# Expert rows of a two-layer kernel: loaded as exchanged 32x32 blocks and turned by VectorE, tags in loads of their own

## The reference

```python
logits = xn @ moe_gate_w + moe_gate_b
topw, topi = jax.lax.top_k(logits, K)                      # 2 of 8 experts per token
topw = jax.nn.softmax(topw, axis=-1)
w_dense = jnp.sum(jax.nn.one_hot(topi, E) * topw[..., None], axis=-2)
h = _gelu(jnp.einsum('bsd,edh->ebsh', xn, ew1) + eb1[:, None, None, :])
eo = jnp.einsum('ebsh,ehd->ebsd', h, ew2) + eb2[:, None, None, :]
moe_out = jnp.einsum('ebsd,bse->bsd', eo, w_dense)
```

## Time and profile before

| | |
|---|---|
| median of 3 runs | 793.02 us (789.99 to 794.43) |
| the profiled execution | 790.34 us |
| its span | 788.4 us |
| busy in the span | TensorE 84%, VectorE 75%, ScalarE 57%, GpSimd 31% |
| first load of a tile issued | 496.64 us |
| `up` of the last tile starts | 719.3 us |

### The profile page before, as it was taken

One profiled execution on the slowest core, in us unless ns is written; L12 is line 12 of the kernel. 1 busy time (PEld: TensorE's weight loads), 2 busy tenths in 40 slices (PEclk: granted clock), 3 DMA queues, 4 the chain that ended last, 5 costly groups with the idle time before them and its releaser, 6 DMA issues. The chain is left out here.

```text
span 788.4 us, 16245 instructions
## 1 busy us (share of the span) xinstructions
PE 662.5 (84%) x4681; PEld 491.2 (62%) x4682; DVE 592.2 (75%) x1649; ACT 452.1 (57%) x868; POOL 244.9 (31%) x295
## 2 busy tenths in 40 slices
PE   5799579999899989989997999599999999999000
PEld 4685335647465564746554687488888889887000
DVE  5836878889797988989789779376767767675493
ACT  3126357573746557384664744467676766765287
POOL 2000202121706335080523354033434333334132
PEclk9999799999999999999998999799999999999555
DMA  4603325253453635335662583454334444220783
GB/s 135 204 0 115 53 80 82 80 108 112 135 115 111 121 121 115 100 111 121 226 125 67 163 282 109 123 149 142 109 116 144 141 145 145 84 82 17 229 280 133
DMA packets 81775, 99.11 MB, mean 126 GB/s; under 512 B 7728, under 2 KB 71867, under 8 KB 81596
## 3 DMA queue, kind: packets, MB, share of 16 engines
q1 hardware_dynamic: 65308, 68.81, 27.9%
q0 software_dynamic: 16416, 29.67, 15.9%
HBM read 62.42 MB, written 33.68 MB: 122 GB/s over the span
## 5 line engine op out<-in xcount | busy, mean ns | idle before, releaser
L1678 POOL DMA_INDIRECT scratch_ys<-ye,place x78 | 83.0, 1064 | 159.7 <-ACT ye L1724 147.8
L52 PE MATMUL bank<-words 128*128 128x512 bf16 (+1 forms) x576 | 109.5, 345 | 8.4 <-DVE words L946 7.4
L52 PE MATMUL down<-words,h_s_e 128*128 x936 | 110.2, 274 | 1.0 <-DVE yb L1799 0.8
L52 PE MATMUL up<-xe_s,words 128*128 128x256 bf16 x936 | 110.1, 275 | 0.9 <-DVE xe_s L1815 0.9
L52 PEld LDWEIGHTS up<-xe_s,words 128*128 x936 | 92.3, 99 | 12.2 <-issue 1.3
L52 PEld LDWEIGHTS down<-words,h_s_e 128*128 128x128 bf16 x936 | 91.2, 98 | 13.9 <-issue 1.5
L52 PE MATMUL bank<-xn_s,mlp_w 128*128 128x512 bf16 x384 | 88.0, 387 | 8.1 <-DVE xn_s L720 8.1
L52 PEld LDWEIGHTS bank<-words 128*128 128x128 bf16 x576 | 55.3, 98 | 56.2 <-DVE words L946 9.1
L462 POOL DMA_INDIRECT scratch_zs<-rows,pos x64 | 73.4, 1147 | 44.3 <-DVE pos L1034 25.5
L52 PE MATMUL bank<-mlp_w,shared 128*128 128x256 bf16 x768 | 86.4, 273 | 0.0
L400 POOL TENSOR_TENSOR rs<-mv,eps_t 128x4 f32<-128x4 f32 x16 | 5.0, 310 | 246.5 <-DVE mv L710 246.5
(11 more groups left out here) (239 smaller groups left out, 1213.4 us busy)
## 6 DMA issues: line engine op xcount, KB each, us to landing
xr<-scratch_zs SPq DMA_DIRECT2D x39, 264.0 KB, 2.9
words<-scratch_ys SPq DMA_DIRECT2D x16, 514.0 KB, 8.8
scratch_abel<-staged SPq DMA_DIRECT2D x8, 514.0 KB, 3.7
abel_all<-scratch_abel SPq DMA_DIRECT2D x8, 514.0 KB, 5.9
x_in<-in_x SPq DMA_DIRECT2D x8, 512.0 KB, 4.9
words<-in_out_b_row SPq DMA_DIRECT2D x8, 512.0 KB, 3.6
x_res<-in_mlp_b_row SPq DMA_DIRECT2D x8, 512.0 KB, 3.6
words<-in_x POOLq DMA_DIRECT2D x8, 512.0 KB, 7.9
```

The lines of the kernel that those rows point to most:

```text
L52: last = nc.tensor.matmul(dst, lhs(a, k), rhs(b, k), start=start and n == 0, stop=stop and n == total - 1)
L1678: nc.gpsimd.indirect_dma_start(out=ys_dram[:, :], out_offset=bass.IndirectOffsetOnAxis(ap=place[:, k, s:s + 1], axis=0), in_=ye[:, k % 2, ...
```

## The change

SyncE loads the data columns of a tile by eight DMAs in place of one. Each takes 32 of the 256 columns for all 256 rows into 32 partitions, as 8 blocks of 32x32, each of which stands where its turned version has to be, but is itself not yet turned. Each contiguous piece is 128 bytes. VectorE then turns all blocks of the tile in one operation (`turned`), into `xt` in SBUF; TensorE's four transposes and their two PSUM banks are gone. VectorE does `turned(q + 2)` at the head of step q.

The tags of four tiles are loaded by four DMAs of their own (`load_tags`), issued right behind the load of every fourth tile, and VectorE makes weights and places of four tiles in one go, in five operations of 128x8, at every fourth step. The buffers for weights and places hold eight tiles, and the loop steps by eight tiles in place of four (4 rounds in place of 8), with `load_branch` twice in it. SyncE waits for `e_xT_done` ahead of a tile and for `e_placed` ahead of tags.

```diff
-        xr = sb("xr", [P, 4, ST, ROW])
+        SQ, GROUP, RING = 32, 4, 8
+        xb = sb("xb", [P, 4, KC, SLOT])
+        xt = sb("xt", [P, 2, KC, SLOT])
+        tags = sb("tags", [P, 2, GROUP, ST, ROW - D])
...
                 row = sp.value_load(tile_row[0:1, bass.ds(q, 1)], min_val=0, max_val=NE * REGION - SLOT)
                 wait(sp, xT_done, q - 3)
-                wait(sp, weight_r, q - 3)
-                wait(sp, placed, q - 3)
-                sp.dma_start(xr[:, k], zs_dram[bass.ds(row, SLOT), :].rearrange("(s p) c -> p s c", p=P))\
-                    .then_inc(zs_in[k], 16)
+                blocks = zs_dram[bass.ds(row, SLOT), 0:D].rearrange("(b j) (k a i) -> a k j b i", j=SQ, k=KC, i=SQ)
+                for a in range(P // SQ):
+                    for c in range(KC):
+                        sp.dma_start(xb[a * SQ:(a + 1) * SQ, k % 4, c].rearrange("j (b i) -> j b i", i=SQ), blocks[a, c])\
+                            .then_inc(zs_in[k % 4], 16)
+                if k % GROUP == 0:
+                    load_tags(q, k // GROUP)
+
+            def load_tags(q, g):
+
+                for n in range(group_size(q)):
+                    row = sp.value_load(tile_row[0:1, bass.ds(q + n, 1)], min_val=0, max_val=NE * REGION - SLOT)
+                    if n == 0:
+                        wait(sp, placed, q - GROUP)
+                    sp.dma_start(tags[:, g, n], zs_dram[bass.ds(row, SLOT), D:ROW].rearrange("(s p) c -> p s c", p=P))\
+                        .then_inc(tags_in[g], 16)
...
-                    nc.scalar.activation(xe[:, k % 2, c], turn_bank[k % 2][:, c], ACT.Identity, bias=beta[:, c:c + 1],
+                    nc.scalar.activation(xe[:, k % 2, c], xt[:, k % 2, c], ACT.Identity, bias=beta[:, c:c + 1],
...
+            def turned(q, k):
+                dve.wait_ge(zs_in[k % 4], (q - k % 4) * 32 + 128)
+                wait(dve, xe_r, KC * (q - 1))
+                nc.vector.transpose(xt[:, k % 2].rearrange("p k n -> p (k n)"),
+                                    xb[:, k % 4].rearrange("p k n -> p (k n)")).then_inc(xT_done, 1)
...
             def body(q, k):
                 if isinstance(q, int) and q == 0:
+                    turned(0, 0)
+                    turned(1, 1)
                     tails(0, 0)
-                places(q, k)
+                if not (isinstance(q, int) and q >= QT - 2):
+                    turned(q + 2, (k + 2) % RING)
+                if k % GROUP == 0:
+                    places(q, k)
...
-            def turned_rows(q, k):
-                pe.wait_ge(zs_in[k], (q - k) * 4 + 16)
-                wait(pe, xe_r, KC * (q - 1))
-                for s in range(ST):
-                    for c in range(KC):
-                        last = nc.tensor.transpose(turn_bank[k % 2][:, c, s * P:(s + 1) * P],
-                                                   xr[:, k, s, c * P:(c + 1) * P], ident[:, :])
-                last.then_inc(xT_done, 1)
-
...
-                if isinstance(q, int) and q == 0:
-                    turned_rows(0, 0)
-                if not (isinstance(q, int) and q == QT - 1):
-                    turned_rows(q + 1, (k + 1) % 4)
                 up(q, k, expert_of(q))
```

More of the change, by code:

```diff
@@ L1581, in experts @@
         xe_s = sb("xe_s", [P, 2, 2 * KC, SLOT], BF16)
-        is_first, more, at = sb("is_first", [P, 4, ST]), sb("more", [P, 4, ST]), sb("at_e", [P, 4, ST])
-        weight = sb("weight", [P, 4, ST])
-        place = sb("place", [P, 4, ST], U32)
+        is_first, more, at = [sb(n, [P, GROUP, ST]) for n in ("is_first", "more", "at_e")]
+        weight = sb("weight", [P, RING, ST])
+        place = sb("place", [P, RING, ST], U32)
         h_s = sb("h_s_e", [P, 2, 2, FC, SLOT], BF16)
@@ L1620, in experts, with group_size @@
         assert TAIL // 4 - 1 == BATCHES
+        def group_size(q):
+            return min(GROUP, QT - q) if isinstance(q, int) else GROUP
         def over_tiles(eng, body, first=0, last=QT, every_four=lambda q: None):
[L1625 to L1630, removed]
+            for q in range(first, GROUP):
+                body(q, q)
+            with eng.Fori(GROUP, TAIL - RING + 1, RING) as q:
+                for k in range(RING):
+                    if k % GROUP == 0:
+                        every_four(q + k)
+                    body(q + k, (GROUP + k) % RING)
             for q in range(TAIL, last):
-                body(q, q % 4)
+                body(q, q % RING)
         @block.sync
@@ L1788, in places, with each @@
-                dve.wait_ge(at_r, q + 1)
-                nc.vector.scalar_tensor_tensor(place[:, k], at[:, k], float(NTILES * P),
-                                               nowhere[:, bass.ds(q, 1)].rearrange("p a s -> p (a s)"), ALU.add,
-                                               ALU.max).then_inc(placed, 1)
+                    return tags[:, g, 0:N, :, c - D:c - D + 1].bitcast(dt).rearrange("p q s a -> p q (s a)")
+                def each(v):
+                    return v.rearrange("p (q a) -> p q a", a=1).to_broadcast([P, N, ST])
@@ new lines, in places @@
+                at_k = slice(k, k + N)
+                dve.wait_ge(tags_in[g], (q - k) * 8 + 16 * N)
+                if not (isinstance(q, int) and q < RING):
+                    for n in range(4):
+                        dve.wait_ge(ys_out[n], (q - RING) * 4 * ST + 16 * ST)
+                nc.vector.tensor_tensor(is_first[:, 0:N], tag(FIRST, I32), each(tef[:, bass.ds(q, N)]), ALU.is_equal)\
+                    .then_inc(first_r, GROUP)
+                dve.wait_ge(first_r, q + GROUP)
+                nc.vector.tensor_tensor(more[:, 0:N], is_first[:, 0:N], tag(MORE_W, F32), ALU.mult)\
+                    .then_inc(more_r, GROUP)
```

46 lines of the change are left out of this document (22 added, 24 removed).

## The result

The changed kernel takes a median of 828.0 us (825.2 to 828.9 over four runs) beside 793.6 us (790.0 to 794.4) for the kernel before: 1.044 times, 95% interval 1.041 to 1.047. The forecast was 846.5 us with a range of 808 to 886: the direction and the cause were right, the size was not, since 53.5 us were forecast to be lost and 34.4 were.

The account below looks back on a forecast made before the run. TensorE bound the kernel before; SyncE's queue was to bind after, at 6.9 us a tile. The last `up` 51.5 us later plus 2 for the clock made 53.5; 790.3 + 53.5 = 843.8, plus 2.7 gives 846.5 us, range 808 to 886.

Parts of the forecast that it names:

- TensorE's part: In the experts' stage, four transposes a tile go, 0.44 us for 38 tiles: 16.7 us gained if nothing else binds.
- VectorE's part: One turn of 128x512 a tile takes VectorE from 4.1 to 4.2 us a tile, at worst 4.9, hidden below 5.28.
- The price of a DMA on SyncE: On SyncE's queue each further DMA of a tile takes 0.58 us; each 10 ns of error moves the result 3.5 us.
- first rival: Under 0.40 us a DMA on SyncE, TensorE's products bind again at 5.28 us a tile: 785 us; chance 0.08.
- The rest of the queue: Besides tile DMAs, SyncE's queue has 0.15 us a tile in the loop, tags 1.16 each, branch loads 1.4, eight times.
- The start: SyncE's loads for the stage start at 495.62 us with nothing loaded, and SyncE is the slowest from then on.
- From the last load to the last `up`: At the stage's end, the last DMA is issued at 760.4 us, lands at 762.9, and the last `up` starts at 770.8.
- The clock: TensorE's gaps every four tiles lower its clock; slack pays inside the stage, 0 to 5 us at its end, 2 taken.
- The products bind: TensorE's products bind at 21.1 us for four tiles, last `up` 7.7 us earlier than before: 785 us; chance 0.08.
- The DMA engines bind: At 47 ns a 128-byte piece, DMA engines need 7.8 us a tile: 884 us; chance 0.14, including a mix with SyncE.
- The clock stays down: TensorE stays at 1.2 GHz through the stage and binds at 10.6 us a tile, 413 us for 39; chance 0.01.
- the factor of 19: A tile's strided load grows 19 times on the DMA engines, to 15.8 us a tile, near 1198 us; chance 0.02.

Follow-up runs that it names:

- the one without turns: The kernel before with TensorE's four transposes left out and ScalarE reading the unturned rows: 776.2 us, 0.982 times before.
- four DMAs: The changed kernel with four DMAs a tile in place of eight, in pieces of 256 bytes, with weights laid out to match: 783.9 us, 0.988 times before.
- the moved tags: Kernel with four DMAs a tile, first tags loaded behind tile 2 and the turn of tile 1 behind the subtraction for tile 0: 782.0 us, 0.988.
- the ninth DMA: The changed kernel with one more DMA a tile, into a buffer nobody reads: 861.2 us (1.085 times before), again 862.5 (1.088).
- half pieces: The changed kernel with half of a tile's rows not loaded from tile 4 on, same number of DMAs: 842.6 us (1.060), then 824.4 (1.040).
- tags with each tile: The changed kernel with each tile's tags loaded behind its eight DMAs, same row number, and places made tile by tile: 823.2 us (1.037), then 805.5 (1.018).
- the kernel without scatters: The changed kernel with GpSimd's scatters of the results replaced by a copy of one column: 819.5 us, 1.037 times before.

## Why the prediction was right, and where it was off

**What bounds, and what takes its place.** Right. TensorE bound before; SyncE's queue binds after, without a wait in the stage, with VectorE waiting at the turn and TensorE for `xe_s`. The experiments make this more than a reading: half of the DMAs bring 44 us, half of the pieces 3.6, 39 value loads less 22.5, and a DMA more costs 0.49 us apart from the holds. One sign was off: TensorE was to be busy three quarters of the stage, and is 84% (172.47 of 205 us), since the queue is less slow than forecast.

**TensorE's part.** 16.7 us forecast, 15.7 measured by taking the turns out alone.

**VectorE's part.** The turn was put at 0.7 us between 0.43 and 1.4; it is 0.711. There is no second pass over the data. VectorE is nowhere the bound.

**The price of a DMA on SyncE** is the mis-sized term: "I take 0.58 us for each further DMA". It is 0.50 (mean over the 273 distances inside tiles 0.52, with a few long ones). The 0.08 is nearly all in the instruction: 317 ns for 32 partitions with eight pieces each, where the price was taken from the distance between two loads of the branch, whose instruction takes 0.39 us. The prediction named this difference of forms in favour of its first rival and then didn't move the price. Inside tiles it makes 273 x 0.58 = 158.3 against 142.4 measured, 15.9 us of the error.

**The rest of the queue.** The 20 plain steps from one tile to the next took 1.13 us each, where 1.16 was forecast outside the loop and 1.31 in it: some 3 us less. Tags stand 1.22 us apart, forecast 1.16, and with the branch the two cost some 3 us more. That these cancel is luck. By its terms the forecast had 263.6 us from the first load to the last (264.8 less one value load and one DMA); measured are 247.6, 16.0 less.

**The start.** The first load was issued at 499.4 where the forecast, from the trace of before, had 496.2: 3 us late. Profiles of other kernels in this study, the one without turns among them (which leaves SyncE's queue as it was), have it anywhere from 496 to 501, so I put this down to the run and not to the change.

**From the last load to the last `up`.** Forecast 11.0 us (759.8 to 770.8), measured 10.0 (747.0 to 757.0). Together: 770.8 + 3.2 - 16.0 - 1.0 = 757.0. But the path is not quite the forecast one. The forecast had the last load on it; in the profile VectorE had the `xe_s` of tile 37 ready at 751.1 us, and its `up` started at 751.57, right behind the product before it. From 723.33 us on TensorE sets the pace, and what hangs on the last load comes in 0.4 us ahead of it. The sum holds because the two end nearly level, which the forecast had no reason for.

**The clock.** Behind the 20 us without products it is down, as forecast: `up` takes 4.51 us there, and the stretch from 510 to 530 us was granted 0.77. Behind the eight gaps in the loop it is so only in part: five `up` (at 543, 571, 621, 672 and 723 us) take 4.3 to 4.5 us in place of 2.8, and three, behind gaps of 1.66, 2.83 and 3.26 us, run at full clock, though the gap of 2.87 us ahead of the `up` at 723 had it down. So the length of the gap alone doesn't tell. What it cost was paid out of slack within the stage, as forecast. The 2 us set aside for the end weren't needed: the last gap ended at 723.33 us, its `up` took 1.8 us longer, and behind it the products follow each other without a gap (the chain that ended last).

```profile
723.33 4.46 PE up L52 x24
727.79 2.66 PE down L52 x24
730.45 2.62 PE up L52 x24
...
751.57 2.62 PE up L52 x24
754.18 2.85 PE down L52 x24
757.03 2.62 PE up L52 x24
```

**Median against profile.** The forecast added the 2.7 us by which the median of before lay over its profiled execution. For the changed kernel they are 828.0 and 827.75. So 846.5 - 828.0 = 18.5 is 16.1 of the profile (843.8 against 827.75: 13.8 at the last `up`, the 2 us of the clock, and 0.2 behind it) and 2.4 of this.

**The rivals.** The products bind: no for the changed kernel, since a DMA costs 0.50 us and the rival's condition was "under 0.40 us in all". The version with four DMAs gets the queue below TensorE's 21.1 us for four tiles by their number, gives the 5.28 us a tile that the rival names, and starts its first product at 510.77 us, for which the rival had 511.0. Its end was forecast at 785 us; with four DMAs it is 783.9. The DMA engines bind: no; the share forecast for the harmless case was "near 50%", it is 55%. The clock stays down: no, 1.00 where no gap stands. The trace gives no sign of the factor of 19 that the Trainium skill has for a DMA which transposes by strides ("VectorE: DVE Perf Modes", The three transpose paths): landings got shorter, 1.9 us in place of 2.9. The Trainium skill's rule on many small transfers ("DMA: Bandwidth & Descriptors", Rules for kernel authors) agrees in its direction; what this case adds is that the queue that issues them is what is paid, and not the DMA engines.

## What to carry to other kernels

Where a DMA is cut into several, count instructions on the queue that issues them, value loads included, and set that against the time of one step: here eight DMAs cost 0.50 us each, with 32 KB or with 16, and four of 64 KB turned a loss of 4.4% into a gain of 1.2%. Take the price from the row nearest in shape (the number of partitions), not merely nearest in place. And when an operation is moved later in a queue, look at everything that stands behind the wait it then has, as the moved tags showed.

## What was not expected of the hardware

**In these traces the issue of a DMA takes a time that goes with its form, and not with its bytes.** 317 ns for 32 partitions with eight pieces each, unchanged with four (half of the bytes) and unchanged with pieces of 256 bytes; 378 ns for 128 partitions with two pieces of 1056 bytes; 389 ns for 128 partitions with two pieces of 32 bytes.

**Pieces of 128 bytes are cheap on the DMA engines.** The share of the DMA engines in a full stretch of 100 us went from 0.40 to 0.57 while packets of under 512 bytes over the whole program went from 7,728 to 102,576:

```profile
DMA packets 166646, 99.21 MB, mean 120 GB/s; under 512 B 102576, under 2 KB 156731, under 8 KB 166460
```

A load of a tile lands sooner after its issue than the single large one, 1.9 us in place of 2.9.

**SyncE's queue was held on one chip, and on two others not.** All five runs on one chip show it (the ninth DMA twice, half pieces, tags with each tile, four DMAs), at two different times: the queue was held about 0.70 us at a time. In the four whose queue never waits for a buffer this makes 46 to 54 gaps of over 0.15 us, 24 to 27 us together. In the seven runs on two other chips no load of rows is recorded with less than 316 ns. Two kernels ran on both kinds of chip: 842.6 against 824.4, and 823.2 against 805.5, 18 us each; the kernel before has 793.0 and 792.7 there and 791.9 and 792.9 elsewhere, since its queue isn't the bound. In the first run with half pieces, 32 of the 33 gaps over 0.4 us between the first load and the last begin within 0.9 us after the start of one of GpSimd's indirect DMAs (13 within 0.11 us, 19 from 0.71 on), though such moments make only a quarter of the stage; in the first run of tags with each tile it is 30 of 31. That they cause the holds is only argued: the kernel without scatters ran on a chip that doesn't show holds at all. What makes that chip different stays open. What follows for the work: here two kernels bound by SyncE's queue differed by 2% from chip to chip, where the kernel before, bound by TensorE, didn't, and a comparison between two runs of such kernels has to look at the shortest instruction of the queue first.
